# A product of bias and weights made mostly on GpSimd, two TensorE products of ones in place of eight, and a new order of the steps

## The reference, cut to what matters

```
block 0:  z  = mha(x, x, Wq1, Wk1, Wv1, mask0, causal)        # 16 heads of 8
          x1 = layernorm(x + z)
          z  = mha(x1, context, Wq2, Wk2, Wv2, mask1)
          x2 = layernorm(x1 + z)
          x3 = layernorm(x2 + ffn(x2))                          # 128 -> 128 -> 128
block 1:  qh, kh, vh = x3 @ wq + bq, ctx @ wk + bk, ctx @ wv + bv   # 16 heads of 64
          scores = qh kh^T / 8 + 2 * fside
          out = layernorm(softmax(scores) vh @ wo + bo + x3)
```

## Time and profile before

| | us |
|---|---|
| median of 3 runs | 341.96 (341.45 to 343.37) |
| profiled execution, its time | 341.61 |
| profiled execution, its span | 339.8 |
| TensorE busy | 320.3 |
| VectorE busy | 291.3 |
| ScalarE busy | 239.9 |
| GpSimd busy | 241.6 |

### The profile page before, as it was taken

How to read it: one execution, slowest core, us unless ns; L and a number is a source line. 1 busy time by engine, 2 the same in 40 slices (tenths; PEclk the granted TensorE clock), 3 DMA queues, 4 the chain that set the end, 5 groups by cost and what they waited for, 6 DMA issues and landing times.

```text
span 339.8 us, 13231 instructions
## 1 busy us (share of the span) xinstructions
PE 320.3 (94%) x5328; PEld 252.3 (74%) x5333; DVE 291.3 (86%) x836; ACT 239.9 (71%) x567; POOL 241.6 (71%) x376
## 2 busy tenths in 40 slices
...
PEclk9999999999999999999999999999999999999998
...
GB/s 154 332 327 210 3 0 2 3 65 4 2 4 133 2 4 2 88 57 12 54 4 3 2 141 4 11 3 33 103 2 5 0 143 3 3 17 136 2 2 31
DMA packets 13180, 17.87 MB, mean 53 GB/s; under 512 B 1601, under 2 KB 10177, under 8 KB 13121
## 3 DMA queue, kind: packets, MB, share of 16 engines
...
...
## 4 chain that ended last, share of the span: by engine, by line
PE 56%; DVE 26%; ACT 5%; issue 5%; POOL 4%; DMA 1%; SPq 1%; POOLq 0%; ACTq 0%; DVEq 0%
PE C_E L632 5%; PE C_E L577 4%; PE B_E L451 3%; PE C_E L622 3%; PE A_E L432 3%; PE B_E L432 3%; PE C_E L593 2%; DVE A_mx L889 2%; PE A_E L451 2%; DVE A_S L897 2%; PE C_E L609 2%; PE B_E L465 2%; DVE Sc L973 2%; DVE C_den L991 2%; DVE L_xh L943 2%
## 5 line engine op out<-in xcount | busy, mean ns | idle before, releaser
L1025 POOL TENSOR_TENSOR A_kblk<-A_qk,cst 128x1024 f32<-128x1024 f32 x16 | 30.3, 1897 | 25.5 <-DVE A_qk L865 25.4
L1046 POOL TENSOR_TENSOR L_xg<-L_xh,vec_sb 128x128 f32<-128x128 f32 x64 | 29.2, 456 | 15.9 <-DVE L_xh L943 13.9
L1035 POOL TENSOR_TENSOR L_rstd<-L_ve,cst 128x1 f32<-128x1 f32 x64 | 35.1, 548 | 5.0
L1077 POOL TENSOR_TENSOR Sc<-Sc,C_mx 128x512 f32<-128x512 f32 x28 | 29.1, 1046 | 9.4 <-DVE C_mx L983 9.3
L763 ACT ACTIVATE qT<-C_E,bq 128x128 f32<-128x128 f32 x112 | 31.9, 379 | 4.1 <-PE C_E L577 3.9
L1033 POOL TENSOR_TENSOR L_ve<-L_mv,cst 128x1 f32<-128x1 f32 x64 | 12.1, 189 | 29.4 <-DVE L_mv L930 28.8
L1086 POOL TENSOR_TENSOR Pc<-Pc,C_rd 128x512 f32<-128x512 f32 x28 | 29.0, 1043 | 2.8 <-DVE C_rd L993 2.5
L1025 POOL TENSOR_TENSOR B_kblk<-B_qk,cst 128x1024 f32<-128x1024 f32 x16 | 30.3, 1897 | 0.0
L577 PE MATMUL C_E<-x3T,wq_sb 128*128 128x128 f32 x224 | 29.6, 279 | 0.4 <-ACT x3T L755 0.4
L577 PEld LDWEIGHTS C_E<-x3T,wq_sb 128*128 128x128 f32 x224 | 27.0, 192 | 1.1 <-ACT x3T L755 0.7
L632 PE MATMUL C_E<-wo_sb,C_zT 128*128 128x128 f32 x224 | 27.5, 276 | 0.1
...
## 6 DMA issues: line engine op xcount, KB each, us to landing
...
```

The costliest lines, as they stand in the source:

```text
L1025: tt(a.kblk[:], a.qk[:, 1].unsqueeze(1).to_broadcast([P, 8, P]), at["rmask"].unsqueeze(2).to_broadcast([P, 8, P]), ALU.mult).then_inc(a.s_ ...
L1035: tt(l.rstd[:], l.ve[:], at["power"], ALU.pow).then_inc(l.s_rstd, 1)
L1046: tt(l.xg[:], l.xh[:], l.g, ALU.mult).then_inc(l.s_xg, 1)
L1077: tt(v, v, place(n).mx[:, 8 * g:8 * g + 8].unsqueeze(2).to_broadcast([P, 8, S]), ALU.subtract).then_inc(C.s_sub, 1)
```

## The change: what it does

- A new step C.bvw on GpSimd multiplies wo_sb by bv, broadcast along the 128 columns (128x1024), into own[0].P, then adds the upper half to the lower (128x512), and again (128x256). Each of the three waits for the one before it.
- C.bvo waits for these instead of the loads, and makes two products with a tile of ones in place of the eight.
- The table of constants has one column of ones more.
- COOL is 7 in place of 6.
- PLAN is replaced as a whole. It has the same steps with C.bvw#0 and three more words of L.warm (two of which do nothing, since COOL is 7). The order of most steps moves by a few places on each engine.

```diff
-COOL = 6
+COOL = 7
-CONST = dict(ident=P, ..., eps0=1, eps1=1)
+CONST = dict(ident=P, ..., eps0=1, eps1=1, ones=1)
...
             def bvo(n):
                 if n:
                     return
-                pe.wait_ge(w_out, 16 * 2)
+                pe.wait_ge(bvw_ready, 3)
                 pe.wait_ge(C.s_vs, 2 * FIRST)
-                for j in range(J):
-                    last = mm(own[0].E[0][:, 0:D], bv_sb[:, j:j + 1].to_broadcast([P, P]), wo_sb[:, j],
-                              start=(j == 0), stop=(j == J - 1))
+                for j in range(2):
+                    last = mm(own[0].E[0][:, 0:D], at["ones"].to_broadcast([P, P]), own[0].P[:, j * D:(j + 1) * D],
+                              start=(j == 0), stop=(j == 1))
                 last.then_inc(bvo_ready, 1)
...
+            def bvw(n):
+                pool.wait_ge(w_out, 16 * 2)
+                w = own[0].P
+                tt(w[:].rearrange("p (j d) -> p j d", d=D), wo_sb[:], bv_sb[:].unsqueeze(2).to_broadcast([P, J, D]),
+                   ALU.mult).then_inc(bvw_ready, 1)
+                pool.wait_ge(bvw_ready, 1)
+                tt(w[:, 0:4 * D], w[:, 0:4 * D], w[:, 4 * D:8 * D], ALU.add).then_inc(bvw_ready, 1)
+                pool.wait_ge(bvw_ready, 2)
+                tt(w[:, 0:2 * D], w[:, 0:2 * D], w[:, 2 * D:4 * D], ALU.add).then_inc(bvw_ready, 1)
```

More of the change, by code:

```diff
@@ L1104 @@
 PLAN = """
[L1105 to L1134, removed]
@@ L1140 @@
[L1140 to L1154, removed]
```

276 lines of the change are left out of this document (161 added, 115 removed).

## The result

The changed kernel takes 344.11 us (median of 17 runs, 343.38 to 346.99) against 341.72 us (17 runs, 341.45 to 343.37) for the kernel before on the same chip. The ratio is 1.0073, its 95% interval 1.0061 to 1.0086: slower by 2.4 us. The forecast was 341.4, no change, with 338.2 to 343.9 for 8 in 10. Of all runs in this text one fell into a slow state, 395.77 us at a mean granted clock of 0.76 (old code in the new order), and is left out. The profiled execution took 343.38 us, its span 341.6.

What follows compares the result with a forecast made beforehand. TensorE and VectorE were taken to bound the kernel by turns. Terms -0.8 + 0 + 0.5 - 0.4 + 0.1 + 0 = -0.6 us against the profiled 341.61 gave 341.0, median 341.4 us; 8 in 10 for 338.2 to 343.9.

Steps and rivals of the forecast that it cites:

- the middle of the new order: The reordered steps between start and end: same instructions, both engines nearly full, taken as 0, bounded by 2.6 us either way.
- The sign that I had set for this: TensorE's and VectorE's idle time, 60 to 300 us, differing by over 2 us would mean the list made the time.
- C.bvo, -0.8 us: TensorE before 61 us: eight products become two, of which -0.8 us is kept, ends -1.5 and 0.
- TensorE's part in the two engines' share of the chain, 56 of 82: Factor for C.bvo: the part of the 1.2 us left on TensorE that is kept, giving -0.8 us.
- VectorE takes it all: Rival: C.bvo gains 0 because VectorE bounds the stretch behind 61.18 us; 342.2 us, chance 0.16.
- C.bvw, 0: GpSimd behind B.kblk#0: three new instructions, together 3.6 us, fit in a 5.37 us idle gap; cost 0.
- The start, +0.5: First 26 us: VectorE's changed order, A.zn#0 sooner for -0.4 and a clash for +0.9; range -0.4 to +1.3.
- The clash: At the start, C.wvlo on VectorE and A.gb#0 on GpSimd delay each other: +0.9 us, ends 0 and +1.2.
- The end, -0.3: Last part of the kernel: -0.4 us from replacing L.warm#4, +0.1 from L.warm#3 and L.warm#6 in waits for ScalarE.
- the gain from L.warm#4: At the end on TensorE, C.pt_0#13 takes the place of these idle products: -0.4 us (0 to -0.6).
- They can bring nothing, as the clock is up until the last slice: At the end, L.warm#3 and L.warm#6 bring no gain in TensorE's clock and cost +0.1 us, ends 0 and +0.3.
- The slower rival: Rival: late C.gb#0 to C.gb#3 on GpSimd hold VectorE's C.xh; 345.1 us, chance 0.20 including other losses of the list.

Runs made afterwards that it cites:

- e1: The changed kernel's code in the order of the kernel before, with C.bvw#0 added right behind B.kblk#0; 341.62 us, ratio 0.9998 to the kernel before.
- e7: The changed kernel's code in the order of before, with only the last 264 words (from about 283 us) in the new order; 342.49 us, ratio 1.0029.
- e11: The changed kernel's code in the order of before, with only the first 61 us (to A.e#4) in the new order; 342.58 us, ratio 1.0023.
- e9: The changed kernel with three words, C.xh#5, C.xh#8 and C.xh#10, moved earlier to avoid starting beside long GpSimd instructions; 343.27 us, ratio 1.0031.

## Why the prediction was wrong

**The step that failed is the middle of the new order, "No row prices it ... I take 0".** One word in it costs 1.3 to 1.4 us of the 2.4: C.xh#8 beside A.kblk#15, shown from both sides, put in and taken out. Rows held its price. The earlier trace rows had the 1.90 us of A.kblk and the earlier trace rows the 0.96 us that wk_lo lost beside GpSimd. I used that for C.wvlo at the start and not for the other VectorE instruction of this kind: C.xh of the last norm, the one of the four that reads l.y and rstd from SBUF, 16 times. In the old order they took at most 0.76 us. The rule of the Trainium skill (SBUF — State Buffer, Who interferes with whom) that I had cited gives just this: of two instructions that need the shared reads, the one that comes second waits for all of the first. The trace agrees, L941 ended 0.15 us after A.kblk. The sign that I had set for this, idle time of the two engines from 60 to 300 us more than 2 us from before, didn't show it: TensorE's is 5.66 against 4.56 us, VectorE's 16.06 against 15.88, 1.3 us in sum.

**C.bvo, -0.8 us: 0.** Removed were 1.34 us (2.02 to 0.68; predicted 1.51). The step "TensorE's part in the two engines' share of the chain, 56 of 82" mis-sized it: a share over the span says nothing of the next hand-over. The earlier trace rows had it: the chain goes to VectorE 0.7 us behind the start of A.qkv, and VectorE starts there at 61.17 as before. The rival "VectorE takes it all" was right in this step. Whether the two products gave anything in the new order isn't shown: the medians are 0.8 us apart (344.93 and 344.11, on different chips), the ratios 0.0005 with intervals that overlap. The bank of C.v_1#3 held TensorE up for 0.17 us ahead of C.x3t#0, for the estimated 0.3.

**C.bvw, 0: right.** 3.89 us for the estimated 3.6; the two sums took 1.27 and 0.73 where I had 1.04 and 0.65. The new code in the old order costs nothing.

**The start, +0.5.** A.zn#0 began at 20.55, not 20.0: VectorE waited 0.95 us for A.z#0, which began at 20.13 in place of 19.55, since it now stands behind K.warm#4 and C.k_1#1 on TensorE. The clash made A.gb#0 1.30 us long (forecast 0.46 + 0.9). In the profiled executions of the changed kernel and of the start alone all of this was made good by 73 us. The start alone is 1.0 us above e1 in its median of 11 runs, 0.8 by its ratio (0.7 between the medians with the idle products, whose intervals overlap). What makes this isn't shown. One thing that I had not seen is: moving K.warm#0 and #1 leaves TensorE idle for 1.9 us and its matmuls run slow behind it, at a cost of 0 to 2.3 us. In the rest of the new order the old start brought nothing (344.70).

**The end, -0.3: +0.9.** No run shows the gain from L.warm#4. What the part costs isn't put down to one place: it has TensorE's waits of 0.76 and 0.51 us and GpSimd's C.gb#12 and C.rstd#13 too late, and undoing either way brought little. In e7's trace C.o#15 starts 0.35 us later than in e1's (332.72 against 332.37 us), and the last C.y then waits another 0.6 us for x3r: the 0.9. "They can bring nothing, as the clock is up until the last slice" was read from one execution; in that of e11 it falls at the end, for 1.6 us.

**The slower rival** (C.gb#0 to #3 late, from 61 to 120 us) did not happen: VectorE did not wait for L_xg before 331 us. The time came out near its 345.1 us by another mechanism, with GpSimd in it; that it did is luck. Its bar of 2.6 us was also too high, as 343.7 less 341.4 is 2.3.

**What stays open.** In the profiled executions the account closes: 343.38, less 1.3 for the one word (342.08), less 0.5 for the other moves (341.56), against 341.61. These are single executions, and that of e9, between the last two, took 343.23 with a stop of 1.15 us in it. In the medians 1.0 us of the 2.4 remains with everything mended. Events of chance were seen in these orders, of 0.9 to 2.8 us each: slow matmuls at the start, the clock at 61 us and at the end, and the stop at 160 us. That the new order makes those other than the first likelier is an inference, from the medians and from four of ten against none of eight; the kernel before has high runs of its own, how often each event comes wasn't measured, and what stops TensorE at 160 us isn't known. The best ratio of all is that of the new code in the old order with idle products at the end, 341.64 against 341.88 us, and its interval touches 1.
